# VectorE takes the first quad's inner pairs of batches 1, 4, 8 and 11 in place of 1, 6 and 11

## What is computed

```python
e = jnp.stack([tbl_f[ids[:, f]] for f in range(16)], axis=1)      # B x 16 x 256
xk = e
for i in range(3):
    z = jnp.einsum('bfe,bge->bfge', e, xk).reshape(B, 256, 256)   # all pairs of fields
    z = jax.nn.relu(jnp.einsum('bcl,oc->bol', jnp.swapaxes(z, 1, 2), Ws[i]) + bs[i][None, :, None])
    z = jnp.sum(z, axis=-1)                                       # B x 16, goes to the output
    xk = jnp.broadcast_to(z[:, :, None], (B, 16, 256))
h = jnp.concatenate([z1, z2, z3, dense_ctx], axis=1)
h = relu(h @ W_top1 + b_top1); h = relu(h @ W_top2 + b_top2); y = h @ W_top3
```

## Time and profile before

| | us |
|---|---|
| median of 3 runs | 578.62 |
| lowest and highest | 578.22, 579.26 |
| the profiled execution, its own time | 579.74 |
| its span in the trace | 578.0 |
| DVE busy | 542.8 |
| ACT busy | 498.7 |
| PE busy | 476.3 |
| POOL busy | 467.8 |
| mean granted TensorE clock, share of full | 0.956 |

### The profile page before, as it was taken

How to read it: one execution, slowest core, us unless ns; L and a number is a source line. 1 busy time by engine, 2 the same in 40 slices (tenths; PEclk the granted TensorE clock), 3 DMA queues, 4 the chain that set the end, 5 groups by cost and what they waited for, 6 DMA issues and landing times.

```text
span 578.0 us, 10773 instructions
## 1 busy us (share of the span) xinstructions
PE 476.3 (82%) x3990; PEld 190.8 (33%) x3990; DVE 542.8 (94%) x326; ACT 498.7 (86%) x1471; POOL 467.8 (81%) x354
## 2 busy tenths in 40 slices
PE   5559888687888798878989788798869888789988
PEld 5213233232333333232333323233333323233324
DVE  1697999999999999999999999999999999999994
ACT  1143698999999999999999999989999999999875
POOL 6665888889888888888888889888888888888630
PEclk9689898999989989998999999799999989999979
DMA  3352212221222122212221222212212212210000
GB/s 98 92 145 74 75 56 57 63 64 56 74 58 64 56 71 72 67 56 74 62 64 56 69 60 61 73 57 82 64 56 66 61 60 74 57 54 1 1 2 0
DMA packets 14334, 35.43 MB, mean 61 GB/s; under 512 B 5493, under 2 KB 5879, under 8 KB 14266
## 3 DMA queue, kind: packets, MB, share of 16 engines
q0 software_dynamic: 12288, 33.57, 20.3%
q1 hardware_dynamic: 1994, 1.17, 0.8%
HBM read 34.71 MB, written 0.01 MB: 60 GB/s over the span
## 4 chain that ended last, share of the span: by engine, by line
DVE 38%; ACT 28%; PE 18%; issue 10%; POOL 3%; another core or an unknown queue 1%; DMA 1%; ACTq 0%; DVEq 0%; POOLq 0%
DVE prod L436 32%; ACT outer L637 15%; PE z_ps L827 8%; DVE outer L485 6%; ACT outer L627 3%; ACT sq L582 3%; POOL x_rows L342 3%; PE t_ps L790 3%; ACT relu L593 2%; ACT xt L574 2%; PE turn_ps L898 1%; PE turn_ps L902 1%; PE turn_ps L860 1%; PE zs_ps L842 1%
## 5 line engine op out<-in xcount | busy, mean ns | idle before, releaser
L436 DVE TENSOR_TENSOR prod<-t_ps,xt 128x2048 f32<-128x2048 f32 x190 | 420.8, 2281 | 11.0 <-remote 6.7
L342 POOL DMA_INDIRECT x_rows<-in_tbl,ids_sb x256 | 248.4, 970 | 73.1 <-issue 62.0
L637 ACT ACTIVATE outer<-outer,bias_sb 128x256 f32<-128x256 f32 x476 | 236.7, 518 | 3.0 <-DVE outer L485 3.0
L827 PE MATMUL z_ps<-prod,w_sb 128*32 128x512 f32 x1520 | 191.2, 622 | 37.3 <-DVE prod L436 34.3
L356 POOL TENSOR_TENSOR intra<-xt 128x1024 f32<-128x1024 f32 (+4 forms) x90 | 205.1, 2281 | 6.0 <-PE z_ps L827 4.5
L574 ACT ACTIVATE xt<-t_ps 128x512 f32<-128x512 f32 x128 | 75.2, 604 | 45.2 <-PE t_ps L790 21.7
L637 ACT ACTIVATION_READ_ACCUMULATOR outer<-outer,bias_sb 128x1 f32 x476 | 100.2, 210 | 0.0
L485 DVE TENSOR_TENSOR outer<-y_ps,z_all 128x1408 f32<-128x1408 f32 (+2 forms) x60 | 93.4, 1598 | 4.5 <-ACT outer L627 3.5
L790 PE MATMUL t_ps<-ident,x_rows 128*128 128x128 f32 x512 | 81.2, 288 | 19.0 <-DMA x_rows<-in_tbl,ids_sb 7.1
L827 PEld LDWEIGHTS z_ps<-prod,w_sb 128*32 128x32 f32 x1520 | 45.8, 111 | 124.8 <-issue 93.3
L790 PEld LDWEIGHTS t_ps<-ident,x_rows 128*128 128x128 f32 x512 | 55.9, 143 | 81.8 <-issue 59.6
(11 more groups left out here) (69 smaller groups left out, 219.1 us busy)
## 6 DMA issues: line engine op xcount, KB each, us to landing
x_rows<-in_tbl,ids_sb POOLq DMA_INDIRECT x256
w_sb<-in_w SPq DMA_DIRECT2D x1, 512.0 KB
feat<-in_dense SPq DMA_DIRECT2D x1, 128.0 KB
w_sb<-in_w SPq DMA_DIRECT2D x1, 128.0 KB
ids_sb<-in_ids SPq DMA_DIRECT2D x1, 120.0 KB
ident<-in_identity SPq DMA_DIRECT2D x1, 64.0 KB, 2.1
w_sb<-in_w0t SPq DMA_DIRECT2D x1, 64.0 KB
sel_sb<-in_sel SPq DMA_DIRECT2D x1, 48.0 KB
```

The lines of the kernel that those rows point to most:

```text
L342: pool.indirect_dma_start(out=x_rows[:, par, f, :], out_offset=None, in_=tables[f], in_offset=bass.IndirectOffsetOnAxis(ap=ids_sb[:, NF * ...
L436: dve.tensor_tensor(prod[:, m % PROD_RING, half, :].rearrange("p (f g s) -> p f g s", f=QF, g=QF), t_ps[:, tbank(b, q, half), :, :].unsque ...
L637: act.activation(outer_of(b)[:, o // OP, o % OP, :], outer_of(b)[:, o // OP, o % OP, :], ACT.Relu, bias=bias12_sb[:, layer - 1, o:o + 1], ...
L827: mm = pe.matmul(z_ps[j * GR:(j + 1) * GR, m % 2, 0:n], w0_sb[:, half, slot, :], src[:, half, j * n:(j + 1) * n], start=(slot == 0 and hal ...
```

## The change

The tuple of the batches whose quad 0 DVE makes is altered. Nothing else is.

```diff
-VECTOR_INNER = (1, 6, 11)
+VECTOR_INNER = (1, 4, 8, 11)
```

## The result

| | before | after |
|---|---|---|
| median, us (12 runs of each, side by side) | 578.42 | 583.83 |
| lowest and highest | 574.37, 582.3 | 579.52, 588.7 |
| the profiled execution, its own time | 579.74 | 583.15 |
| its span | 578.0 | 581.0 |

The changed kernel is slower. The ratio is 1.0077 with an interval of 1.0043 to 1.0111, which is +4.5 us (+2.5 to +6.4). Foretold were 580.1 and at most 582.2. The ratios, and the levels fitted further down, leave disturbed runs out, so a ratio need not be the quotient of the two medians.

What follows compares the result with a forecast made beforehand. DVE was taken to bound the steady part, with only 5.50 us idle. Terms 1.80 - 1.10 + 1.80 - 1.00 = +1.50 us took the median from 578.62 to 580.1, range 577.9 to 582.2.

Steps and rivals of the forecast that it cites:

- the collision in frame 4: Rival: POOL's product slips between DVE's shared instructions, DVE waits 1.28 us, sum +2.78; chance 0.14 for frame 4 or 8.
- Direction: Whole kernel: slower 0.55, same 0.37, faster 0.08; sum of the terms +1.50 us.
- Frame 4, +1.80: Three shared instructions added on DVE in a frame without idle time, delaying all behind them by 1.80 us.
- The two ends the port rule left open: Shared pairs in frame 4: +2.78 if the lock is given up between two VectorE instructions, +1.50 if not.
- Frame 6, -1.10: Shared pairs removed from DVE: 1.10 of 1.80 us comes back, the other 0.70 was a covered wait for ACT's slices.
- Frame 8, +1.80: Shared pairs added on DVE, again in a frame without idle time: 1.80 us.
- Given back in frames 9 to 11, -1.00: DVE's 3.19 us idle there shrinks by 1.00 as ACT and PE get ahead: 0.36 in frame 9, 0.64 in 10 and 11.
- The rival that POOL sets the pace of frames 9 to 11: Relieving POOL frees DVE, all 5.50 us idle time goes: -3.70, 574.9 us; chance 0.07.

Runs made afterwards that it cites:

- c_1_6_8_11: Kernel before with batch 8 shared as well, VECTOR_INNER (1, 6, 8, 11); 581.83 us, ratio 1.0073.
- m_1_6_10: Kernel before with its last shared batch moved from 11 to 10, (1, 6, 10); 579.57 us, ratio 1.0032.
- d_1_8_11: Kernel before with shared batch 6 moved to 8, (1, 8, 11); 582.88 us, ratio 1.0065.
- g_two: Kernel before with batch 6 moved to 8 and batch 11 no longer shared, (1, 8); 582.42 us, ratio 1.0039.
- b_1_4_11: Kernel before with shared batch 6 moved to 4, without batch 8, (1, 4, 11); 578.77 us, ratio 1.0026.
- f_five: Changed kernel with batch 6 kept, five shared batches (1, 4, 6, 8, 11); 587.24 us, ratio 1.0089 to the kernel before.
- i_1_6_9_11: Kernel before with batch 9 shared too, (1, 6, 9, 11); 578.66 us, ratio 1.0009.
- n_1_5_9_13: Kernel before with four shared batches, (1, 5, 9, 13), all but the first in frames with an idle DVE; 580.06 us, ratio 1.0013.
- o_after_clear: Changed kernel with POOL's last product of pair 1 behind two more gathers in all four shared frames; 583.85 us, ratio 1.0098 to the kernel before.
- a_clear: Changed kernel with POOL's last product of pair 1 behind two more gathers in frames 4 and 11; 582.98 us, ratio 1.0116 to the kernel before.
- e_force: Kernel before with one gather moved so POOL's middle product of pair 1 falls on the shared pairs of batches 6 and 11; 579.67 us, ratio 1.0022.
- l_clear: Kernel sharing (1, 6, 8, 11) with POOL's order changed so gathers stand beside DVE's shared pairs; 584.04 us, ratio 1.0088 to the kernel before.
- h_pad8: Kernel before with three plain fills of unused y_row on DVE in frame 8, nothing taken off POOL; 581.66 us, ratio 1.0031.
- k_clear: Kernel before with POOL's order changed so gathers stand beside DVE's shared pairs in frames 1, 6 and 11; 580.56 us, ratio 1.0008.

## Why one profile says less than the median

**after_again** and **before_again** are the two kernels unchanged, run once more for a second profile of each.

> The changed kernel once more, for a second trace, since its runs spread from 579.5 to 588.7. If the collision in frame 4 is a matter of the order and not of chance, the group of frame 4 takes over 3 us again (POOL's last product of pair 1 starts 0.1 to 0.4 us behind it); the group of frame 11 may or may not meet a product. If the long groups were chance, 1.9 us in both.

> The kernel before once more, for a second trace. Its runs spread from 574.2 to 585, and fall by 2.4 us for each 0.01 of mean granted TensorE clock. If that spread lies in waits of DVE on ACT behind dips of the clock, frames 5 to 14 of this trace have another sum of idle time than 5.5 us, and frames 1 to 4 and 8 are as before.

after_again: 584.75 (10 runs), and the profiled execution took 588.13 with a span of 586.0, 5.0 more than the first one. before_again: 577.93, ratio 1.0001, span 575.7, 2.3 less than the first. Timeline of DVE of after_again, frames 5 to 7, from the outer products at the end of frame 5 on:

```profile
220.75 2.89 DVE L485 TENSOR_TENSOR outer<-y_ps,z_all 128x1280 f32<-128x1280 f32 x2 [0.84 <-ACT outer L627]
223.56 13.30 DVE L436 TENSOR_TENSOR prod<-t_ps,xt 128x2048 f32<-128x2048 f32 x6
237.13 3.16 DVE L485 TENSOR_TENSOR outer<-y_ps,z_all 128x1408 f32<-128x1408 f32 x2 [0.27 <-ACT outer L627]
240.20 13.27 DVE L436 TENSOR_TENSOR prod<-t_ps,xt 128x2048 f32<-128x2048 f32 x6
254.05 2.89 DVE L485 TENSOR_TENSOR outer<-y_ps,z_all 128x1280 f32<-128x1280 f32 x2 [0.58 <-ACT outer L627]
258.82 4.49 DVE L436 TENSOR_TENSOR prod<-t_ps,xt 128x2048 f32<-128x2048 f32 x2 [1.89 <-ACT xt L574]
```

The same kernel that in its first profile passed frames 5 to 7 at the floor here loses 0.84, 0.27, 0.58 and 1.89 us. The busy times by stretches of after_again (us, then busy PE, PEld, DVE, ACT and POOL with instructions, the granted clock, DMA share, GB/s) show what stands ahead of the long wait, and PE's row in the timeline shows why PE was idle:

```profile
240.00:242.00 2.00, 0.57 (x4) 0.33 (x4) 2.00 (x2) 2.00 (x3) 1.84 (x2) 1.00 0.23 70
242.00:244.00 2.00, 1.50 (x2) 0.50 (x2) 2.00 (x2) 2.00 (x8) 1.68 (x3) 0.50 0.25 74
244.00:246.00 2.00, 2.00 (x9) 0.40 (x12) 2.00 (x2) 2.00 (x8) 2.00 (x1) 0.50 0.24 66
```

```profile
242.50 1.22 PE L894 MATMUL turn_ps<-feat,w_sb 64*128 64x512 f32 x1 [1.93 <-ACT h L658]
```

PE waited 1.93 us for ACT (busy 0.57 of 2.00), and from 242 on the granted clock is 0.50, the lower of its two levels (1.2 GHz). One matmul of line L894 takes 1.22 us there, where two took 1.12 in the same trace at 238.86 with the full clock. PE turns the next rows later, ACT copies them later, and DVE waits 1.89 for `xt` at 258.82. How much of that is the 1.93 us of waiting and how much the lower clock, this trace does not separate. The same is to be seen in the tails of the two profiles of the kernel before, where nothing is different in the program. First before, then before_again, the stretches 550 to 560 and 560 to 570:

```profile
550.00:560.00 10.00, 8.40 (x20) 3.47 (x20) 10.00 (x26) 9.54 (x37) 2.60 (x1) 0.84 0.01 2
560.00:570.00 10.00, 9.97 (x24) 3.50 (x22) 7.69 (x25) 4.74 (x15) 2.46 (x1) 0.82 0.01 2
```

```profile
550.00:560.00 10.00, 8.00 (x29) 3.45 (x30) 9.89 (x23) 9.56 (x38) 2.60 (x1) 1.00 0.01 2
560.00:570.00 10.00, 9.44 (x33) 4.27 (x31) 9.16 (x30) 7.33 (x23) 2.47 (x1) 1.00 0.01 2
```

From the start of frame 15 to the end pass 578.0 - 517.47 = 60.5 us with the dip and 575.7 - 518.48 = 57.2 without it. So one dip there is worth 3.3 us, more than twice the forecast. All 18 profiles bear this out, whatever the kernel: the six without a dip behind the first moments of frame 15 take 57.1 to 57.9 us from there to the end, the ten with one as long as that of the kernel before 60.5 to 61.1, and c_1_6_8_11 and m_1_6_10, whose dip is half as long, 58.9 and 59.4. What PE does just ahead of it is the same in both profiles shown (busy for 0.7 of 2 us), so that alone does not decide whether the clock falls. The dips fall at other places in each execution, and a profile of one execution holds one draw of them. That also is why c can be short in its profile and its median high. Both kernels have these draws, so they widen every comparison and do not explain why the changed kernel is slower in the mean.

before_again shows one thing more. Rows of PE and of DVE in its frame 11:

```profile
389.98 2.79 PE L827 MATMUL z_ps<-intra,w_sb 128*32 128x384 f32 x16 [2.17 <-POOL intra L356]
```

```profile
399.90 3.15 DVE L485 TENSOR_TENSOR outer<-y_ps,z_all 128x1408 f32<-128x1408 f32 x2 [2.18 <-ACT outer L627]
```

PE waited 2.17 us for POOL's inner pairs of i1, and 9.92 us later DVE waited 2.18 for ACT's slices; the chain that ended last in this trace runs through POOL's gathers and its product there. The same pair of waits stands in d_1_8_11 (1.86 at 290.61, 1.76 at 300.42) and in g_two (1.87 at 456.91, 1.88 at 466.82). In all three the granted clock is down to 0.50 just behind PE's wait, and the traces do not part its share from that of the wait. So in some executions POOL, late with i1, sets DVE's pace for some 2 us, in the kernel before too, although its first trace has no such place.

## Why the prediction was wrong, step by step

- **Direction.** Slower with a chance of 0.55, and the mechanism for it, that DVE bounds the steady part and the two groups go straight onto the path in frames 4 and 8, was right. The size was not: +1.5 foretold; measured +4.5 by the ratio and +5.0 ± 0.5 by the fit. With what the traces show put in, the collision of 1.45 and the 0.37 outside the span, the sum would have been +3.3, and with nothing given back +4.3, which is within the error of the measurement. So three terms failed: the collision, put at nothing; the time outside the span, put at nothing without a reason; and perhaps what is given back.
- **Frame 4, +1.80.** The work was right. The term lacked 1.45 of collision. That was named as a rival of 0.14, with the right place and price (1.28), and argued down by the step "DVE was there first by 0.5 us and POOL waited for all three instructions in the one case with the same instructions". That step failed: the case was a gather, not a product. Moreover the lead was 0.28 and not 0.5: DVE came 0.38 later than foretold, POOL 0.12. In eight places of these traces a product of POOL started while one of the shared instructions was recorded as running, 0.25 to 0.36 us after its start (frame 4 of after, after_again, b and f_five, frame 11 of i, frames 5 and 9 of n, frame 1 of o_after_clear). In all eight the group took 3.29 to 3.43 us, and POOL's product kept its 1.28 to 1.30. What this costs in the whole time is open (frame lengths show 1.45, the timed runs anything from nothing to that). What a lead of 0.5 would have done no trace shows. POOL waits as at 84.72 when its instruction is a gather; the same is to be seen at 183.01 of a_clear, 1.14 instead of 0.95. The case in the tail, where the instruction of DVE took 2.69, was the one that resembled this and should have had the weight.
- **The two ends the port rule left open.** The prediction drew on the Trainium skill, page "SBUF — State Buffer", section "SBUF: two separate sides": exclusive, and whoever starts first keeps it. Exclusive holds here. "Starts first" does not hold if the start in the trace is meant: in all eight places DVE's record starts first and POOL goes first. Where DVE's first instruction (0.95 long when alone) was hit, in five of the eight places, it ended 0.82 after POOL's product, and it ends 0.82 or 0.83 after it also where POOL's product had begun first (0.42 us ahead in frame 11 of after, 1.29 in frame 6 of e_force). In the other three the third one (0.41 alone) was hit and ended 0.29 after. So it had nearly all of its work before it when POOL was through, as if it had not taken the ports up to 0.36 us after its recorded start; the traces cannot show that moment.
- **Frame 6, -1.10.** 1.84 in the first profile; waits of 0.58 and 0.89 in after_again and b. Batch 6 was worth 0.8 ± 0.8 in the timed runs. Right within what can be told.
- **Frame 8, +1.80.** Right as DVE's length in that frame (34.04). As a cost of the kernel it was set too low: +3.1 ± 0.6 (c), and after against b says 3.4 ± 0.7, both with the 0.37 outside the span in them. Plain work of the same length there costs 2.1 ± 0.6, with the same 0.37. Whether a further 1 us or so is real is not shown, and where it would come from is open. It is not the collisions (l_clear). What is left is POOL's other pace: its short instructions let it run ahead (12.9 us idle ahead of its inner pairs instead of 6.0), so its gathers and products fall elsewhere. I have no run that separates that from the clock, and no run with POOL's short instructions alone was tried.
- **Given back in frames 9 to 11, -1.00.** Not settled. In the profile 0.77 of idle time went and the collision of frame 11 took 0.74, which leaves 0.03. The timed runs of h_pad8 fit with nothing given back and do not exclude 1.00. With shared pairs and collisions taken off, frames 9 to 11 idle from 1.55 us (b) to 4.41 (before_again) where nothing delays DVE in frame 8, and from 0.95 (c) to 4.57 (l_clear, d_1_8_11) where batch 8 does: the scatter of single profiles is larger than the term. The waits of frames 9 and 10 on ACT's slices did stay, as foretold. Frame 13 lost its wait of 0.94 instead; as such waits come and go between two profiles of one kernel, that cannot be put down to the change.
- **POOL.** In the trace of the prediction it does not set the pace, and with the change PE's waits for POOL's inner pairs went (0.8 before, none after) without the kernel getting faster. But 0.8 us was one draw: before_again has 4.2, of which 2.17 came out as a wait of DVE. The rival that POOL sets the pace of frames 9 to 11 was right for that execution and wrong in sign for the change.
- **The range.** It was made from the mechanisms alone. The clock's share was missing: the frames and the tail of a single profile were taken as fixed numbers, while two profiles of the same kernel differ by 2.3 and 5.0 us. The 0.37 outside the span was missing too, and the collision stood in the range only in place of other terms and not on top of its upper end, 582.2.

No kernel tried is faster than the one before; i_1_6_9_11, k_clear and n_1_5_9_13, and by their ratios also b_1_4_11, e_force and h_pad8, cannot be told from it.

## What to carry to other kernels

When work moves from GpSimd to VectorE, look at what stands on GpSimd at the very time at which the new instructions run: an elementwise product there makes VectorE wait its whole length, even where VectorE's record starts 0.3 us earlier, and a gather does not. Put the extra work where the receiving engine waits for a third one anyway; here the fourth shared batch cost 0.4 ± 0.6 us in such a frame and 3.1 ± 0.6 in a full one. And before a prediction is summed to a tenth of a microsecond, take two profiles of the same kernel: where the granted clock dips at changing places, their difference is the least error to put on the sum.

## What the runs showed of the hardware

- VectorE's two-input instruction that starts 0.25 to 0.36 us ahead of GpSimd's is not protected by that: 2.36 to 2.47 us instead of 0.95 in five places, 1.89 to 1.90 instead of 0.41 in three, with GpSimd's at its full speed. Against a gather it is the other way round (1.76, 1.53, 1.14 us instead of 0.95 for the gather, nothing for VectorE).
- The run time goes with the mean granted clock of TensorE even though VectorE is the busiest engine: 2.0 ± 0.2 us for 0.01, as a correlation. One trace shows a way: ACT's copies of what PE has turned come late (1.89 <-ACT xt), and VectorE waits. In the tail a dip lengthens 57.2 us to 60.5, in 18 profiles without exception.
- The time of an execution outside the span of its instructions differs between programs by 0.37 us (1.80 and 2.17), steadily in all runs of each; why is open.
